# Attention 2 up to unit 93: the value sums of a head pair in one block on TensorE

## Chip, cores and metric

One core of one Trainium2 chip runs the whole program. The metric is device time in microseconds (us) of one execution, the median of several runs.

## What is computed

Two transformer-like layers with adaptive layer norm. Layer 0 is a sliding-window attention and a feed-forward with low-rank updates; layer 1 is a latent attention ("Attention 2" here) and a second feed-forward. The part that matters is the attention of layer 1, with B = 2 batches, S = 512 rows, 128 heads, 4 value columns per head and 64 rope columns:

```
q_c = (c_q @ Wq_up).reshape(b, s, N_HEADS, HEAD_DIM)
q_r = (x @ Wq_rope).reshape(b, s, N_HEADS, ROPE)
scores = (einsum('bqhd,bkhd->bhqk', q_c, k_c) + einsum('bqhd,bkd->bhqk', q_r, k_r)) / scale
attn = softmax(scores, axis=-1)
out = einsum('bhqk,bkhd->bqhd', attn, v_c)
```

## The kernel before

Each engine runs a program of its own, in the order in which it is written, and semaphores tie them together; no scheduler moves anything. Attention 2 works in **units**: unit u is one head pair (two heads) of one batch, pair u // 2, batch u % 2. There are 128 units (UNITS). Up to unit 95 (HALVED = 96) the exponentials of key tiles 0 to 2 are split into two fp16 parts for the value sums; the last key tile stays fp32. From unit 96 on all value sums are fp32.

TensorE's program is a row of **turns**. Turn u holds, in this order (`before_sums`, `behind_sums`):

- the scores of unit u for slots 0 to 3: for each slot a rope matmul (`scores1_rope`, line 2593) and a content matmul (`scores1_content`, line 2600) into bank s % 4. Between them stand `maximum` 0 and 1 (line 2578), which compute approximate scores of unit u + 2, a quarter of a head's queries each, into banks 4 and 5 in turn (their row maxima shift the exponentials later);
- `sum_unit`: the value sums of unit u - 1 into bank 7 (lines 2623 and 2628): 12 matmuls with fp16 data of 512 columns, then 4 with fp32 data of 256 columns. Each matmul writes one of four groups of 32 rows;
- slots 4 to 7 of unit u, `maximum` 2 to 7, and in four pieces the rope queries of unit u + 3 (`queries`, lines 2508 to 2510, 12 matmuls) into bank 6.

In short: 16 score matmuls, 8 of the maxima and 12 of the queries, 36 full ones in each turn, and the block of value sums after the 12th of them. Below r, c, m and q stand for rope, content, maximum and query matmul, so the turn reads r0 c0 r1 c1 r2 c2 r3 m0 c3 m1, the block, r4 c4 m2 q(3) m3 r5 c5 q(3) m4 r6 c6 q(3) m5 r7 c7 m6 q(3) m7.

VectorE (`period`, `maxima`) does in turn u: `q_low` of unit u + 2 (lines 1886 and 1887, the low part of the queries, once ScalarE's `q_high` and so bank 6 are done); then for each of the 8 maxima a reduction over a whole bank (line 1934), after which that bank may be written again; after reductions 4 and 5 `unit_low` (line 1925), the low fp16 part of slots 4 and 5; in even turns after reduction 1 the high part of rope weights (line 1807); at the end a transpose (line 1946). TensorE's side of the two banks is one wait in `max_scores`:

```
wait(pe, max_done, 8 * w + i - 1)
pe.matmul(bank[4 + i % 2][:], q2[:, k % 4, h, i % 4:S:4], km[:, b, h], ...).then_inc(max_mm, 1)
```

So maximum 2 waits until reduction 0 of the same turn is done. `unit_low` waits for the exponential of the slot that follows next:

```
dve.wait_ge(exp1, 8 * u + s + 6)
```

ScalarE does `q_high` (lines 1373, 1374), the 8 exponentials (line 1413), the high fp16 part of slots 4 and 5 (line 1420) and of slots 2 and 3 (line 1424), and in even turns the copy of bank 7 to `ost` (line 1408). GpSimd does both fp16 parts of slots 0 and 1, the low part of slots 2 and 3 (lines 923, 925, 934), three-part bf16 values (`values`, lines 905 to 915) and in even turns the low part of the rope weights (line 850). SyncE issues the DMAs of each turn.

`pv1` counts value sums that are done, `p_split` and `p_low` the fp16 parts, `exp1` the exponentials.

Of the kernel before, what the change touches and what calls it, by code (L numbers as in the profile page):

```python
# [34 lines left out]
UNITS = PAIRS * B  # L35
# [36 lines left out]
def adaln_two_layers(nc, a, out):  # L72
# [8 lines left out]
    with ctx:  # L81
# [638 lines left out]
        def _(pool):  # L720
# [176 lines left out]
            def values(v, k, pair):  # L897
# [5 lines left out]
                wait(pool, pv1, v - 1)  # L903
# [13 lines left out]
            def halve(u, k, pair):  # L917

                par = k % 2
                for i in range(2):  # L920
                    pool.wait_ge(exp1, 8 * u + 5 + i)
# [6 lines left out]
                if k % 2 == 0:  # L928
                    split_rope_weights(pair(4), (k // 2) % 2)
                if not (isinstance(u, int) and u == HALVED - 1):  # L930
                    values(u + 1, k + 1, pair(1))
                pool.wait_ge(exp1, 8 * u + 9)
# [10 lines left out]
            values(0, 0, 0)  # L943
            for u in range(6):
                turn(u, u % 4, lambda n, u=u: (u + n) // 2)
# [145 lines left out]
        def _(act):  # L1091
# [284 lines left out]
            def period(u, k, pair):  # L1376
# [11 lines left out]
                for s in range(8):  # L1388
# [20 lines left out]
                    if exists(u, UNITS):  # L1409
                        in_place = s in IN_PLACE and exists(u, HALVED)  # L1410
                        act.wait_ge(scores1, 8 * u + s + 1)
                        wait(act, pv1, u - 1)
# [8 lines left out]
                    if s == 3 and exists(u, HALVED):  # L1421
                        act.wait_ge(exp1, 8 * u + 8)
                        for i in (2, 3):
# [726 lines left out]
        def _(pe):  # L2150
# [450 lines left out]

            def sum_unit(w, k, pair):

                if exists(w, UNITS):
# [6 lines left out]
                    if isinstance(w, int) and w == 0:  # L2611
                        pe.wait_ge(gate_ready, 6)
                    halved = exists(w, HALVED)
                    apart = isinstance(w, int) and w >= DIRECT
                    opens, closes = apart or k % 2 == 0, apart or k % 2 == 1
                    rows = lambda group: bank[7][32 * group:32 * group + 32, :]
                    if halved:
                        pe.wait_ge(p_split, 4 * w + 4)
                        pe.wait_ge(p_low, 2 * w + 2)
                        for kb in range(HTILES):  # L2620
                            for h in range(2):
                                for half in range(2):
                                    pe.matmul(rows(2 * h + half), vpb[:, k % 2, kb, h], halved_part(k % 2, SLOTS.index((h, kb)), half),  # L2623
                                              start=(kb == 0 and opens), stop=False)
                        for h in range(2):
                            for half in range(2):
                                at = slice(half * S // 2, (half + 1) * S // 2)
                                e = pe.matmul(rows(2 * h + half)[:, at], vp[:, k % 2, HTILES, h], PT[k % 2][:, SLOTS.index((h, HTILES)), at],  # L2628
                                              start=False, stop=closes)
# [296 lines left out]
```

## Time and profile before

| what | us |
|---|---|
| runs, median of 3 | 2178.25 (2177.45 to 2180.17) |
| profiled execution, its own time | 2175.61 |
| span of the profiled execution | 2173.8 |
| TensorE busy | 2122.4 (98%) |
| VectorE, ScalarE, GpSimd busy | 1732.3, 1341.9, 1357.7 |

Turns with fp16 value sums run from about 828 to 1757 us. A matmul's row has the start at which it entered the array and a modelled end; the time that one costs is the distance to the next start. A row "x8" merges instructions that follow each other.

### The profile page before, as it was taken

The page shows a single profiled execution, that of the slowest core. Times are in us where ns is not written, and L with a number is a line of the kernel's source. Part 1 is how long each engine was busy: PE and PEld are TensorE (multiplying, and loading weights), DVE is VectorE, ACT ScalarE, POOL GpSimd, SP SyncE. Part 2 cuts the span into 40 slices and gives each one's busy share as a digit, 9 for nine tenths or more (in the row PEclk, how much of TensorE's full clock was granted, in tenths as well). Part 3 has the DMA queues.
Part 4 walks back from the last instruction along what each step waited for, and adds up shares of the span by engine and source line. Part 5 has one row for each costly group of instructions (what it writes and reads, how often), then busy time and mean ns, then how long its engine had stood idle before and what let it go on. Part 6 is the DMA issues. An engine that isn't in the chain of part 4 may idle for free.

```text
span 2173.8 us, 42824 instructions
## 1 busy us (share of the span) xinstructions
PE 2122.4 (98%) x11276; PEld 1644.1 (76%) x11276; DVE 1732.3 (80%) x3095; ACT 1341.9 (62%) x2709; POOL 1357.7 (62%) x1621
## 2 busy tenths in 40 slices
PE   7999999999999999999999999999999999999978
PEld 4788888888886757777777777777777777777756
DVE  6787788788777758888888888888888877788764
ACT  2443443433433568888888888888888865555532
POOL 4766766766753447777777777777777721365334
PEclk9999999999999999999999999999999999999999
DMA  7010010010004153222222222222222222444441
GB/s 249 26 43 30 20 48 29 19 48 29 19 20 121 37 189 108 71 73 78 74 78 65 77 78 74 76 66 79 75 77 69 75 79 76 138 130 124 114 130 40
DMA packets 138991, 165.82 MB, mean 76 GB/s; under 512 B 30261, under 2 KB 72917, under 8 KB 138916
## 3 DMA queue, kind: packets, MB, share of 16 engines
q1 hardware_dynamic: 135076, 152.31, 24.5%
q0 software_dynamic: 3840, 12.59, 2.0%
q8 instruction: 37, 0.61, 0.1%
q14 instruction: 38, 0.31, 0.0%
HBM read 101.52 MB, written 29.10 MB: 60 GB/s over the span
## 4 chain that ended last, share of the span: by engine, by line
PE 87%; DVE 7%; issue 2%; ACT 1%; POOL 1%; SPq 1%; DMA 1%; DVEq 0%; ACTq 0%; POOLq 0%
PE bank L2593 12%; PE bank L2578 11%; PE bank L2600 11%; PE bank L2155 7%; PE bank L2157 7%; PE bank L2156 7%; PE bank L2510 6%; PE bank L2508 5%; PE bank L2509 5%; PE bank L2623 3%; PE bank L2633 3%; PE bank L2628 2%; DVE rope_b L1631 1%; DVE rope_a L1630 1%; DVE rope_b L1632 1%
## 5 line engine op out<-in xcount | busy, mean ns | idle before, releaser
L1934 DVE TENSOR_REDUCE mcol<-bank 128x1 fp32r<-128x512 f32 x1024 | 684.1, 687 | 186.8 <-PE bank L2578 176.7
L2593 PE MATMUL bank<-q,k 128*128 128x512 f32 x1024 | 417.9, 408 | 0.0
L2578 PE MATMUL bank<-km,q 128*128 128x512 f32 x1024 | 406.0, 397 | 3.5 <-ACT q L1374 2.5
L2600 PE MATMUL bank<-q,k 128*128 128x512 f32 x1024 | 404.0, 395 | 0.0
L2578 PEld LDWEIGHTS bank<-km,q 128*128 128x128 f32 x1024 | 317.6, 310 | 53.0 <-DVE mcol L1934 3.9
L1413 ACT ACTIVATE pT<-bank 128x512 f32<-128x512 f32 x416 | 228.1, 602 | 113.7 <-PE bank L2600 111.9
L1413 ACT ACTIVATE x<-bank 128x512 f32<-128x512 f32 x416 | 227.7, 601 | 88.7 <-PE bank L2600 86.5
L2593 PEld LDWEIGHTS bank<-q,k 128*128 128x128 f32 x1024 | 192.3, 188 | 84.7 <-issue 27.9
L2600 PEld LDWEIGHTS bank<-q,k 128*128 128x128 f32 x1024 | 192.9, 188 | 31.7
L2510 PE MATMUL bank<-hT_hi,wr_lo 128*128 128x512 f32 x512 | 205.5, 401 | 0.0
L2508 PE MATMUL bank<-hT_hi,wr_hi 128*128 128x512 f32 x512 | 202.3, 395 | 0.1
L2509 PE MATMUL bank<-hT_lo,wr_hi 128*128 128x512 f32 x512 | 202.1, 395 | 0.0
L850 POOL TENSOR_TENSOR wr_lo<-wst,wr_hi 128x512 fp32r<-128x512 f32 x64 | 82.5, 1289 | 131.1 <-DVE wr_hi L1807 131.1
L2155 PE MATMUL bank<-hT_hi,w_hi 128*128 128x512 f32 x376 | 150.3, 400 | 0.0
L2157 PE MATMUL bank<-hT_hi,w_lo 128*128 128x512 f32 x376 | 148.5, 395 | 0.0
L2156 PE MATMUL bank<-hT_lo,w_hi 128*128 128x512 f32 x376 | 148.4, 395 | 0.0
L744 POOL TENSOR_TENSOR bq_lo<-rope_a,bq_hi 128x512 fp32r<-128x512 f32 x64 | 83.3, 1302 | 82.0 <-ACT bq_hi L1145 82.0
L923 POOL CAST pH<-x 128x512 f16<-128x512 f32 x96 | 58.8, 612 | 118.6 <-ACT x L1413 118.6
L736 POOL TENSOR_TENSOR rope_a<-rope_a,rope_b 128x512 f32<-128x512 f32 x80 | 105.8, 1323 | 43.2 <-DVE rope_b L1632 43.2
L1925 DVE TENSOR_TENSOR pH_late<-bank,pH_late 128x512 f16<-128x512 f32 x192 | 131.3, 684 | 1.5
L1413 ACT ACTIVATE bank<-bank 128x512 f32<-128x512 f32 x192 | 112.0, 583 | 19.7 <-PE bank L2600 19.7
L925 POOL TENSOR_TENSOR pH<-x,pH 128x512 f16<-128x512 f32 x96 | 117.8, 1227 | 7.7
(372 smaller groups left out, 5061.5 us busy)
## 6 DMA issues: line engine op xcount, KB each, us to landing
q<-q SPq DMA_DIRECT2D x256, 128.0 KB, 2.3
wst<-in_L_attn_Wq_rope SPq DMA_DIRECT2D x64, 256.0 KB, 3.1
o_d<-ost SPq DMA_DIRECT2D x63, 256.0 KB, 3.1
st_q<-in_L_attn_wq SPq DMA_DIRECT2D x8, 1024.0 KB, 7.6
st_wo<-in_L_attn_wo SPq DMA_DIRECT2D x8, 1024.0 KB, 5.4
q<-qc_d SPq DMA_DIRECT2D x256, 32.0 KB
km<-kc_d SPq DMA_DIRECT2D x256, 32.0 KB
k<-kc_d SPq DMA_DIRECT2D x256, 32.0 KB
```

The source lines that it names most:

```text
L1413: act.activation(bank[s % 4][:] if in_place else PT[k % 2][:, s], bank[s % 4][:], ACT.Exp, scale=float((HD1 + ROPE) ** -0.5)).then_inc(exp ...
L1925: dve.tensor_tensor(halved_part(k % 2, s, 1), bank[s % 4][:], halved_part(k % 2, s, 0), ALU.subtract).then_inc(p_low, 1)
L1934: dve.tensor_reduce(mcol[:, k % 2, i % 4, i // 4:i // 4 + 1], bank[4 + i % 2][:], AX.X, ALU.max, negate=True)\
L2155: pe.matmul(ps, lh_, rh, start=(i == 0), stop=False)
L2156: pe.matmul(ps, lh_, rl, start=False, stop=False)
L2157: e = pe.matmul(ps, ll, rh, start=False, stop=(i == n - 1))
L2508: pe.matmul(bank[6][:], wr_hi[:, par, kk], hT_hi[:, kk, at], start=(kk == 0), stop=False)
L2509: pe.matmul(bank[6][:], wr_hi[:, par, kk], hT_lo[:, kk, at], start=False, stop=False)
L2510: e = pe.matmul(bank[6][:], wr_lo[:, par, kk], hT_hi[:, kk, at], start=False, stop=(kk == KT - 1))
L2578: pe.matmul(bank[4 + i % 2][:], q2[:, k % 4, h, i % 4:S:4], km[:, b, h], start=True, stop=True).then_inc(max_mm, 1)
L2593: pe.matmul(bank[s % 4][:], k1[:, k % 2, t], q1[:, k % 4, h], start=True, stop=False)
L2600: pe.matmul(bank[s % 4][:], k2[:, k % 2, h, t], q2[:, k % 4, h], start=False, stop=True).then_inc(scores1, 1)
```

## The change

Up to turn 94 TensorE has no block of value sums in odd turns. In even turns `sum_pair` sums units u - 2 and u - 1 together: both units' fp16 matmuls, then both units' fp32 ones, with one wait on each semaphore in front. From turn 95 on `sum_unit` works as before. The other engines follow: exponentials of slots 0 to 3 wait for GpSimd's splits in place of `pv1`, and what writes into an fp16 part or a value tile waits for the last pair block. In even turns ScalarE does the high part of slots 2 and 3 behind slot 5 in place of behind slot 3. GpSimd does the rope weights first in even turns, then, after the pair block, the splits, then the values of both units. VectorE's and SyncE's code is not touched.

```diff
--- before.py
+++ after.py
@@ -900,7 +900,7 @@
                 full = vc[:, TB * kp:TB * kp + TB, bass.ds(pair * 8, 8)].rearrange("p t (h d) -> p t h d", h=2)
                 src = full[:, 0:HTILES]
                 first, second, third = (vpb[:, kp, 0:HTILES, :, OROWS * kp + i * HD1:OROWS * kp + i * HD1 + HD1] for i in range(3))
-                wait(pool, pv1, v - 1)
+                wait(pool, pv1, v - kp)
                 pool.sem_inc(spare, 1)
                 pool.tensor_copy(first, src).then_inc(vp_ready, 1)
                 pool.tensor_copy(vp[:, kp, HTILES:TB, :, OROWS * kp:OROWS * kp + HD1], full[:, HTILES:TB])
@@ -917,7 +917,10 @@
             def halve(u, k, pair):
 
                 par = k % 2
+                if par == 0:
+                    split_rope_weights(pair(4), (k // 2) % 2)
                 for i in range(2):
+                    wait(pool, pv1, u - par)
                     pool.wait_ge(exp1, 8 * u + 5 + i)
                     pool.sem_inc(spare, 1)
                     pool.tensor_copy(halved_part(par, i, 0), PT[par][:, i]).then_inc(p_split, 1)
@@ -925,11 +928,10 @@
                     e = pool.tensor_tensor(halved_part(par, i, 1), PT[par][:, i], halved_part(par, i, 0), ALU.subtract)
                     if i == 1:
                         e.then_inc(p_split, 1)
-                if k % 2 == 0:
-                    split_rope_weights(pair(4), (k // 2) % 2)
-                if not (isinstance(u, int) and u == HALVED - 1):
+                if par == 0 and not (isinstance(u, int) and u == 0):
+                    values(u, k, pair(0))
                     values(u + 1, k + 1, pair(1))
-                pool.wait_ge(exp1, 8 * u + 9)
+                pool.wait_ge(exp1, 8 * u + (9 if par else 11))
                 for i in range(2, 4):
                     e = pool.tensor_tensor(halved_part(par, i, 1), PT[par][:, i], halved_part(par, i, 0), ALU.subtract)
                 e.then_inc(p_split, 1)
@@ -941,6 +943,7 @@
             pool.wait_ge(vc_ready, NT)
             pool.wait_ge(zeroed, 7)
             values(0, 0, 0)
+            values(1, 1, 0)
             for u in range(6):
                 turn(u, u % 4, lambda n, u=u: (u + n) // 2)
             with pool.Fori(1, LOOP // 4) as g:
@@ -1409,7 +1412,12 @@
                     if exists(u, UNITS):
                         in_place = s in IN_PLACE and exists(u, HALVED)
                         act.wait_ge(scores1, 8 * u + s + 1)
-                        wait(act, pv1, u - 1)
+                        if not exists(u, HALVED):
+                            act.wait_ge(pv1, u - 1)
+                        elif s < 4:
+                            wait(act, p_split, 4 * u - 4)
+                        else:
+                            wait(act, pv1, u - k % 2)
                         act.activation(bank[s % 4][:] if in_place else PT[k % 2][:, s], bank[s % 4][:], ACT.Exp,
                                        scale=float((HD1 + ROPE) ** -0.5)).then_inc(exp1, 1)
                         if in_place:
@@ -1418,8 +1426,9 @@
                                     act.wait_ge(c_stored[i], CONTENT_DMAS[i] * KT)
                             act.wait_ge(exp1, 8 * u + s + 5)
                             act.activation(halved_part(k % 2, s, 0), bank[s % 4][:], ACT.Copy)
-                    if s == 3 and exists(u, HALVED):
+                    if s == (3 if k % 2 else 5) and exists(u, HALVED):
                         act.wait_ge(exp1, 8 * u + 8)
+                        wait(act, pv1, u - k % 2)
                         for i in (2, 3):
                             act.activation(halved_part(k % 2, i, 0), PT[k % 2][:, i], ACT.Copy)
 
@@ -2599,6 +2608,41 @@
                     t = slice(kb * P, (kb + 1) * P)
                     pe.matmul(bank[s % 4][:], k2[:, k % 2, h, t], q2[:, k % 4, h], start=False, stop=True).then_inc(scores1, 1)
 
+            def sum_rows(group):
+                return bank[7][32 * group:32 * group + 32, :]
+
+            def halved_sums(k, opens):
+
+                for kb in range(HTILES):
+                    for h in range(2):
+                        for half in range(2):
+                            pe.matmul(sum_rows(2 * h + half), vpb[:, k % 2, kb, h], halved_part(k % 2, SLOTS.index((h, kb)), half),
+                                      start=(kb == 0 and opens), stop=False)
+
+            def rest_sums(k, closes):
+
+                for h in range(2):
+                    for half in range(2):
+                        at = slice(half * S // 2, (half + 1) * S // 2)
+                        e = pe.matmul(sum_rows(2 * h + half)[:, at], vp[:, k % 2, HTILES, h], PT[k % 2][:, SLOTS.index((h, HTILES)), at],
+                                      start=False, stop=closes)
+                return e
+
+            def sum_pair(u, k, pair):
+
+                if exists(u - 2, UNITS):
+                    pe.wait_ge(exp1, 8 * u + 4)
+                    pe.wait_ge(vp_ready, VP_STEPS * u)
+                    wait(pe, o_copied, pair(-2))
+                    if isinstance(u, int) and u == 2:
+                        pe.wait_ge(gate_ready, 6)
+                    pe.wait_ge(p_split, 4 * u)
+                    pe.wait_ge(p_low, 2 * u)
+                    halved_sums(0, True)
+                    halved_sums(1, False)
+                    rest_sums(0, False)
+                    rest_sums(1, True).then_inc(pv1, 2)
+
             def sum_unit(w, k, pair):
 
                 if exists(w, UNITS):
@@ -2608,29 +2652,17 @@
                         wait(pe, o_copied, pair)
                     elif isinstance(w, int) and w == UNITS - 1:
                         pe.wait_ge(o_copied, PAIRS)
-                    if isinstance(w, int) and w == 0:
-                        pe.wait_ge(gate_ready, 6)
                     apart = isinstance(w, int) and w >= DIRECT
                     opens, closes = apart or k % 2 == 0, apart or k % 2 == 1
...
+                    if exists(w, HALVED):
                         pe.wait_ge(p_split, 4 * w + 4)
                         pe.wait_ge(p_low, 2 * w + 2)
...
+                        halved_sums(k, opens)
+                        e = rest_sums(k, closes)
                     else:
                         for s in range(8):
                             h, kb = SLOTS[s]
...
                     e.then_inc(pv1, 1)
 
             def scores(u, k, pair, slots):
@@ -2654,7 +2686,10 @@
                 maximum(*turn, 0)
                 scores1_content(turn[0], turn[1], 3)
                 maximum(*turn, 1)
-                sum_unit(turn[0] - 1, turn[1] - 1, turn[2](-1))
+                if isinstance(turn[0], int) and turn[0] > HALVED - 2:
+                    sum_unit(turn[0] - 1, turn[1] - 1, turn[2](-1))
+                elif turn[1] % 2 == 0:
+                    sum_pair(*turn)
 
             def behind_sums(*turn):
 
```

**TensorE, the middle of an odd turn in the loop.** Rope and content are rows of q1,k1 and q2,k2, the maxima rows of km,q2 (bank4 is m0 and m2, bank5 m1). Before:

```order
L2578 MATMUL bank4<-km,q2 128x512
L2600 MATMUL bank3<-q2,k2 128x512
L2578 MATMUL bank5<-km,q2 128x512
...
L2623 MATMUL bank7<-pH,vp 32x512 x8
L2623 MATMUL bank7<-pH_late,vp 32x512 x4
L2628 MATMUL bank7<-x,vp 32x256 x4
...
L2593 MATMUL bank0<-q1,k1 128x512
L2600 MATMUL bank0<-q2,k2 128x512
...
L2578 MATMUL bank4<-km,q2 128x512
```

and now, from the same m0 to the same m2:

```order
L2587 MATMUL bank4<-km,q2 128x512
L2609 MATMUL bank3<-q2,k2 128x512
L2587 MATMUL bank5<-km,q2 128x512
...
L2602 MATMUL bank0<-q1,k1 128x512
L2609 MATMUL bank0<-q2,k2 128x512
...
L2587 MATMUL bank4<-km,q2 128x512
```

The second use of bank 4 follows the first after four other matmuls, where the block stood between them before.

**TensorE, the block of an even turn now** (pH and pH_late are the fp16 parts, x and pT the fp32 exponentials of the two units):

```order
L2619 MATMUL bank7<-pH,vp 32x512 x8
L2619 MATMUL bank7<-pH_late,vp 32x512 x4
L2619 MATMUL bank7<-pH,vp 32x512 x8
L2619 MATMUL bank7<-pH_late,vp 32x512 x4
L2627 MATMUL bank7<-x,vp 32x256 x4
L2627 MATMUL bank7<-pT,vp 32x256 x4
```

It holds two blocks' matmuls between one entry and one exit.

**ScalarE, the second half of an even turn.** Before, the copies of slots 2 and 3 (pH<-x x2) stand ahead of slot 4:

```order
L1424 ACTIVATE pH<-x 128x512 x2
...
L1408 ACTIVATE ost<-bank7 128x512
...
L1413 ACTIVATE bank1<-bank1 128x512
...
L1420 ACTIVATE pH_late<-bank1 128x512
...
L1413 ACTIVATE x<-bank2 128x512
```

and now between slot 5 and the exponential of slot 6:

```order
L1411 ACTIVATE ost<-bank7 128x512
...
L1421 ACTIVATE bank1<-bank1 128x512
...
L1428 ACTIVATE pH_late<-bank1 128x512
...
L1433 ACTIVATE pH<-x 128x512 x2
...
L1421 ACTIVATE x<-bank2 128x512
```

The exponential of slot 6 is two instructions later on its engine.

## Rows read from the trace of the kernel before

**Rows 1.** Busy time in the stretch of fp16 turns; columns named in the view.
```profile
core 0: us, PE busy (x) PEld busy (x) DVE busy (x) ACT busy (x) POOL busy (x), PEclk, DMA share, GB/s
828.25:1746.75 918.50, 918.50 (x5265) 717.63 (x5264) 792.33 (x1268) 761.94 (x1362) 693.95 (x1081) 1.00 0.28 75
```

**Rows 2.** Timeline, TensorE, around two blocks: start us, length us, what.
```profile
1199.68 0.61 PE L2623 MATMUL bank<-pH,vp 128*32 128x512 f16 x8
...
1205.17 0.39 PE L2578 MATMUL bank<-km,q 128*128 128x512 f32 x1
...
1209.14 0.40 PE L2578 MATMUL bank<-km,q 128*128 128x512 f32 x1
1209.46 0.62 PE L2623 MATMUL bank<-pH,vp 128*32 128x512 f16 x8
1209.91 0.39 PE L2623 MATMUL bank<-pH_late,vp 128*32 128x512 f16 x4
1210.12 0.60 PE L2628 MATMUL bank<-pT,vp 128*32 128x256 f32 x8
1210.66 0.50 PE L2593 MATMUL bank<-q,k 128*128 128x512 f32 x1
...
1211.24 0.39 PE L2578 MATMUL bank<-km,q 128*128 128x512 f32 x1
```

**Rows 3.** Chain of work that ended last, at a block: start us, us on it.
```profile
1209.54 0.76 PE bank L2623 x12
1210.30 0.43 PE bank L2628 x8
1210.73 0.43 PE bank L2593
```

**Rows 4.** Timeline, VectorE, from reduction 5 of a turn to the next turn's start.
```profile
1205.60 0.69 DVE L1934 TENSOR_REDUCE mcol<-bank 128x1 fp32r<-128x512 f32 x1
1206.21 0.68 DVE L1925 TENSOR_TENSOR pH_late<-bank,pH_late 128x512 f16<-128x512 f32 x1
1206.81 1.28 DVE L1934 TENSOR_REDUCE mcol<-bank 128x1 fp32r<-128x512 f32 x2
1208.12 0.41 DVE L1946 STREAM_TRANSPOSE mrow<-mcol 128x128 f32<-128x128 f32 x1
1208.56 0.68 DVE L1886 TENSOR_TENSOR q<-bank,q 64x512 fp32r<-64x512 f32 x1
1209.26 0.69 DVE L1887 TENSOR_TENSOR q<-bank,q 64x512 fp32r<-64x512 f32 x1
1209.99 1.29 DVE L1934 TENSOR_REDUCE mcol<-bank 128x1 fp32r<-128x512 f32 x2
1211.31 0.43 DVE L1807 CAST wr_hi<-wst 128x512 fp32r<-128x512 f32 x1
```

**Rows 5.** Timeline near the end of Attention 2: a maximum that waits for a reduction.
```profile
2062.10 1.29 DVE L1934 TENSOR_REDUCE mcol<-bank 128x1 fp32r<-128x512 f32 x2 [1.21 <-PE bank L2578]
...
2062.84 0.31 PEld L2578 LDWEIGHTS bank<-km,q 128*128 128x128 f32 x1 [0.52 <-DVE mcol L1934]
2062.84 0.63 PE L2578 MATMUL bank<-km,q 128*128 128x512 f32 x1
...
2063.31 0.39 PE L2593 MATMUL bank<-q,k 128*128 128x512 f32 x1
```

**Rows 6.** Timeline, ScalarE, in an even turn.
```profile
1210.33 1.15 ACT L1424 ACTIVATE pH<-x 128x512 f16<-128x512 f32 x2
...
1213.05 0.58 ACT L1413 ACTIVATE bank<-bank 128x512 f32<-128x512 f32 x1
1213.66 0.60 ACT L1420 ACTIVATE pH_late<-bank 128x512 f16<-128x512 f32 x1
```

**Rows 7.** Timeline, GpSimd, in the same even turn: first, wr_lo and last instruction.
```profile
1209.00 0.61 POOL L923 CAST pH<-x 128x512 f16<-128x512 f32 x1 [2.52 <-ACT x L1413]
...
1212.72 1.29 POOL L850 TENSOR_TENSOR wr_lo<-wst,wr_hi 128x512 fp32r<-128x512 f32 x1
...
1215.33 2.29 POOL L934 TENSOR_TENSOR pH<-x,pH 128x512 f16<-128x512 f32 x2
```

**Rows 8.** Busy time and clock in a stretch of layer 0 with TensorE idle at times.
```profile
666.00:680.00 14.00, 9.91 (x50) 7.89 (x50) 8.66 (x22) 4.26 (x13) 7.44 (x6) 1.00 0.73 275
```

More of the change, by code:

```diff
@@ L2610, in sum_unit @@
                         pe.wait_ge(o_copied, PAIRS)
-                    if isinstance(w, int) and w == 0:
-                        pe.wait_ge(gate_ready, 6)
-                    halved = exists(w, HALVED)
                     apart = isinstance(w, int) and w >= DIRECT
                     opens, closes = apart or k % 2 == 0, apart or k % 2 == 1
-                    rows = lambda group: bank[7][32 * group:32 * group + 32, :]
-                    if halved:
+                    if exists(w, HALVED):
                         pe.wait_ge(p_split, 4 * w + 4)
                         pe.wait_ge(p_low, 2 * w + 2)
[L2620 to L2629, printed above, removed]
+                        halved_sums(k, opens)
+                        e = rest_sums(k, closes)
                     else:
@@ L2632, in sum_unit @@
                             h, kb = SLOTS[s]
-                            e = pe.matmul(rows(2 * h + kb % 2), vp[:, k % 2, kb, h], PT[k % 2][:, s], start=(s < 4 and opens), stop=(s >= 4 and closes))
+                            e = pe.matmul(sum_rows(2 * h + kb % 2), vp[:, k % 2, kb, h], PT[k % 2][:, s], start=(s < 4 and opens), stop=(s >= 4 and closes))
                     e.then_inc(pv1, 1)
```

## The prediction

> **What bounds the kernel now.** I began with the busy table by stretch. In the fp16 turns TensorE is busy for all of 918.50 us, at full granted clock (1.00, the 2.4 GHz level); VectorE has 792.33, or 86% of it, ScalarE 83% and GpSimd 76% [rows 1]. So TensorE sets the pace of this stage, with VectorE close behind, and what the change is worth is read from TensorE's distances between starts.
>
> Next, TensorE's timeline. From one block of value sums to the next it is 1209.46 - 1199.68 = 9.78 us, one turn [rows 2]. From m5 at 1205.17 to m1 at 1209.14 lie 17 full matmuls, 3.97 us, so one costs 0.2335. The 36 of a turn make 8.41, which leaves 1.37 for the block. The chain says the same at the block itself: 0.76 for the fp16 matmuls, 0.43 for the fp32 ones, and 0.43 in place of 0.23 for the r4 behind them, 1.39 in all [rows 3]. Of this the work itself is 1210.12 - 1209.46 = 0.66 and 0.43 [rows 2, 3]. The other 0.28 to 0.30 is a price for entering and leaving the block, paid once per block: a late first load, and a slow restart of the full-width matmuls.
>
> Last, VectorE's timeline over the border of two turns. Reduction 5 starts at 1205.60, 0.43 after its maximum m5 [rows 2, 4]. From there VectorE never waits: unit_low, reductions 6 and 7, the transpose, two halves of q_low, reductions 0 and 1 follow on each other's heels. Reduction 0 starts at 1209.99 and takes 0.69, so it ends at 1210.68, 5.51 us after m5 started. In the same turn m2, which needs that bank, started at 1211.24 [rows 2]. The slack was 0.56 us. It is this slack that the change touches.
>
> **The change, part by part.**
>
> *The pair block.* It holds two blocks' work and one entry and exit: 1.38 + 0.66 + 0.43 = 2.47 us in place of 2 x 1.38 = 2.76. Gain 0.29 per pair. All of it lies on TensorE's path. The bounds: nothing, if the fp16 and fp32 halves of the second unit pay an entry of their own (0.29 again), and 0.30 by the chain's figures. I take 0.29, because inside the old block the fp32 part starts right when the fp16 part is through (0.45 and 0.21 us between the three starts of rows 2, which is 12 matmuls in 0.66 with no gap).
>
> *The odd turn loses its block, and with it 1.38 us between m1 and r4.* VectorE's code is the same, so its chain from m5 of the even turn to the end of reduction 0 of the odd one remains 5.51 us. On TensorE m5 to m2 is now 20 matmuls (r7 c7 m6, three q, m7, r0 to c2, r3 m0 c3 m1, r4 c4) with nothing else between: 20 x 0.2335 = 4.67. So m2 must wait. How long such a wait is, the end of Attention 2 shows: reduction 0 starts at 2062.10, ends 0.69 later at 2062.79, and m2 starts at 2062.84, with VectorE named as its releaser; the next matmul starts 0.47 behind it and not 0.23, because the weights of m2 are only loaded then [rows 5]. So the price is 5.51 + 0.05 - 4.67 = 0.89 of waiting and 0.47 - 0.23 = 0.24 of restart, together **1.13 us per odd turn**. After it TensorE runs free: m3 comes 0.93 + 0.24 behind, reduction 1 ends 0.60 after reduction 0, and m5 and VectorE keep their old distance. In the even turn the block of 2.47 stands between m1 and m2, and m2 has more slack than before.
>
> *Bounds of that price.* From below: the weights could be loaded during the wait, 0.24 less, so 0.89. Less than that, down to nothing, needs a shorter chain on VectorE, whose instructions do not change. From above: the chain starts late. Its second link, unit_low of slot 5, needs the exponential of slot 6, and in even turns ScalarE now has the two copies of slots 2 and 3 ahead of that. From the start of exponential 5: 0.61 to the second fp16 copy, 0.60 for it, 1.15 for the two moved copies, 0.58 for exponential 6, together 2.94 us [rows 6]. VectorE wants it 10 matmuls after (c5 to m5, 2.33) plus 0.61 (reduction 5), also 2.94 us [rows 4]. This falls level. I take zero, and let the bound be 0.3 us.
>
> *GpSimd.* It gets later starts, not more work. One unit is 8.62 us from 1209.00 to 1217.62, with 1.29 for wr_lo [rows 7], so 7.33 without it and 14.7 for two. In an even turn wr_hi is ready at 4.70 us after r0: reduction 0 starts at 2.95 (m5 + 4.82, less the 8 matmuls from m5 to r0, 1.87), reduction 1 ends 1.29 later, the cast takes 0.43 [rows 4]. wr_lo ends at about 6.1, both units are split at 20.8. The next pair block is due one pair of turns (20.4) plus 2.4 later, at 22.8. So 2.0 us of slack: hidden. If that cover were gone, each microsecond over it would be a microsecond per pair.
>
> *ScalarE and SyncE.* ScalarE waits in even turns for the block's end (2.47 + 2.4 = 4.9 us into the turn) and then does `ost` and slot 4, whose scores arrive 0.6 later; its total work is unchanged. The exponentials of slots 0 to 3 are written before the block ends, as they now wait for the splits only. SyncE's queue issues the same transfers in the same order, and by the code each is used about a turn or more after its issue. Zero for both.
>
> *Sum.* Each pair: + 1.13 - 0.29 = + 0.84 us, 19.56 becoming 20.40. There are 47 pair blocks (turns 2 to 94), but turn 0 ahead of the first odd turn holds late gate matmuls as well, which give VectorE time; I let that pair cost nothing (an estimate, worth 0.8 us at most). So 46 x 0.84 = 38.6 us. The profiled execution took 2175.61 (span 2173.8) and becomes 2214.2. The median of the runs, 2178.25, lies 2.6 above it; there I expect **2217 us**, 1.8% slower.
>
> **The rivals.**
>
> *The wait does not bite: faster.* If VectorE's chain from m5 to the end of reduction 0 took 4.6 us or less instead of 5.51, m2 would go straight on and only the 0.29 remained: 47 x 0.29 = 13.6, so 2164.6 us. For it: the slack today is 0.56, and no row of this stage shows such a wait. Against it: the chain has no idle row in it, and 1.38 us are taken out of a path with 0.56 to spare. Chance 7%. That losses and gains meet (a stall of only 0.3 us) has 3%.
>
> *The moved copies make it worse.* If exponential 6 comes 0.3 us late, unit_low and everything behind it shift, and the pair costs 0.84 + 0.30 = 1.14: 46 x 1.14 = 52, so 2231 us. It decides from the first tenth, as the sum above is level. Chance 14%.
>
> *GpSimd becomes the bound.* With 2 us more in its chain than its rows add up to, the pair block waits for `p_split`. A late arrival by 1 us gives 46 x 1.84 = 85, so 2263 us. For it speaks that nothing of its two turns' work but wr_lo can start before the pair block; against it the 2.0 us of slack. Chance 3%.
>
> *The clock drops.* In the stretch around 670 us TensorE was idle for 4.1 of 14 us and the granted clock stayed 1.00 [rows 8]. Were it to fall to the 1.2 GHz level for a whole turn of each pair, 8.41 us would be added 47 times, near 400 us and 2610 in all. The Trainium skill, page "TensorE: Matmul & The Clock Gate", section "A second HAM failure mode: psum-queue depth-cycling", speaks against this change: a matmul stream that cycles through PSUM banks and idles briefly and often can swing between the two clock levels. By that rule the time would be this rival's; the stretch above had such gaps and does not bear it out. Chance 1%.
>
> *That the change doesn't do what it says* has no room: TensorE's order shows the two blocks merged and the odd turn without one.
>
> **How the numbers follow.** The forecast case, a wait of about 0.9 plus the restart in each odd turn, has 72%; the rivals 7, 3, 14, 3 and 1. The likeliest case gives 2217. Its own bounds are 0.60 to 1.0 per pair: 28 to 46 us, 2206 to 2224. To leave out no more than 2 in 10 the range takes in the moved copies above (2231) and, below, 0.07 us less per pair than the lower bound (3 us): **2203 to 2231**. A measurement of this kernel tells 0.2% (4.4 us) from no change. Faster by more than that: 7%. Within it: 2% (a stall that just eats the gain). Slower: 91%.
>
> **What the profile after should show.** TensorE's fp16 rows in groups of 24 every 20.4 us; from the first fp16 matmul of a block to r4 2.3 us. In odd turns a wait at m2 for VectorE's line 1934, about 46 times and 0.5 to 0.9 us each, with a 0.47 step behind it. VectorE's idle before reduction 2 stays, that before reductions 3 and 4 as well. TensorE's share of busy time falls below 98%, the clock stays 1.00. The forecast is wrong if m2 in odd turns follows c4 by 0.23, or if the waits are at the block (GpSimd) or at r1 (`p_low`).

## The result and the profile after

The changed kernel ("after") takes **2214.81 us** (median; 2213.9 to 2215.68) against 2177.45 for the kernel before in the same session (2174.46 to 2180.17). The ratio is 1.0177, 95% interval 1.0163 to 1.0191: slower by 1.8%, far outside the 0.2% that can be told from no change. The forecast was 2217, with 2203 to 2231 around it. The profiled execution of after took 2214.41 (span 2212.6), 38.8 us more in the span than before's 2173.8. One run of one version below (experiment 3) took 5962.57 us, was slow, and is left out of the comparison.

First the busy table of the stretch of fp16 turns of after; columns as in [rows 1].

```profile
828.00:1785.00 957.00, 923.06 (x5268) 722.24 (x5267) 797.13 (x1269) 760.42 (x1366) 684.57 (x1080) 1.00 0.27 72
```

In [rows 1] TensorE had no idle microsecond in 918.50. Now it is idle for 957.00 - 923.06 = 34 us, at an unchanged granted clock of 1.00 (2.4 GHz). What it waits for, the view of TensorE's waits says (us in total, times, longest), here for 828 to 1757 us:

```profile
PE bank L2587 <- DVE mcol L1943: 32.9, 45, 0.7
```

The same view of before has no row in that stretch. L2587 is `maximum` and L1943 is the reduction (L2578 and L1934 before). In the shares of the chain that ended last, TensorE went from 87% to 71% and VectorE from 7% to 14%:

```profile
PE 71%; DVE 14%; issue 6%; ACT 5%; DMA 1%; POOL 1%; SPq 1%; DVEq 0%; ACTq 0%; POOLq 0%
```

Where it happens is in TensorE's timeline of after over one pair of turns (start, length, what). These rows answer to [rows 2].

```profile
1203.48 0.40 PE L2587 MATMUL bank<-km,q 128*128 128x512 f32 x1
1203.81 0.62 PE L2619 MATMUL bank<-pH,vp 128*32 128x512 f16 x8
...
1205.55 0.60 PE L2627 MATMUL bank<-pT,vp 128*32 128x256 f32 x8
1206.08 0.50 PE L2602 MATMUL bank<-q,k 128*128 128x512 f32 x1
1206.41 0.40 PE L2609 MATMUL bank<-q,k 128*128 128x512 f32 x1
...
1210.36 0.39 PE L2587 MATMUL bank<-km,q 128*128 128x512 f32 x1
...
1214.34 0.39 PE L2587 MATMUL bank<-km,q 128*128 128x512 f32 x1
1214.57 0.40 PE L2602 MATMUL bank<-q,k 128*128 128x512 f32 x1
1214.80 0.39 PE L2609 MATMUL bank<-q,k 128*128 128x512 f32 x1
1215.92 0.62 PE L2587 MATMUL bank<-km,q 128*128 128x512 f32 x1 [0.73 <-DVE mcol L1943]
1216.38 0.39 PE L2517 MATMUL bank<-hT_hi,wr_hi 128*128 128x512 f32 x1
...
1224.17 0.62 PE L2619 MATMUL bank<-pH,vp 128*32 128x512 f16 x8
```

Block to block is 1224.17 - 1203.81 = 20.36 us, where two turns of before took 2 x 9.78 = 19.56 (medians of all pairs: 20.35 and 19.55). A block stands after m1, the tenth full matmul of its turn; the description of the kernel before says the 12th, but its own list r0 to m1 has ten. The first matmul of the pair block to r4 is 2.27. In the odd turn m1, r4 and c4 follow at matmul distance, and then m2 starts 1.12 us behind c4 and the next matmul 0.46 behind m2, in place of 0.23 and 0.23. That is 0.89 and 0.23, or 1.12 us too much per odd turn. (The weights of m2 are loaded from 1215.92 on, at its own start, and those of the matmul behind it from 1216.13 on.) The bracket names 0.73 us of idle time only: c4's modelled end takes up part of the distance, so the distance between starts is the number to sum, not the idle column.

VectorE's timeline of the same turns answers to [rows 4]:

```profile
1210.79 0.69 DVE L1943 TENSOR_REDUCE mcol<-bank 128x1 fp32r<-128x512 f32 x1
1211.40 0.68 DVE L1934 TENSOR_TENSOR pH_late<-bank,pH_late 128x512 f16<-128x512 f32 x1
1212.00 1.28 DVE L1943 TENSOR_REDUCE mcol<-bank 128x1 fp32r<-128x512 f32 x2
1213.31 0.41 DVE L1955 STREAM_TRANSPOSE mrow<-mcol 128x128 f32<-128x128 f32 x1
1213.75 0.69 DVE L1895 TENSOR_TENSOR q<-bank,q 64x512 fp32r<-64x512 f32 x1
1214.45 0.69 DVE L1896 TENSOR_TENSOR q<-bank,q 64x512 fp32r<-64x512 f32 x1
1215.17 2.10 DVE L1943 TENSOR_REDUCE mcol<-bank 128x1 fp32r<-128x512 f32 x3
```

It is the chain of before, link by link, with no idle time in it: m5 at 1210.36 to reduction 0 at 1215.17 is 4.81 us (4.82 before), and with the reduction's 0.69 it ends at 1215.86. m2 starts 0.06 behind that.

The two engines whose work was moved kept up. ScalarE does the two moved copies (L1433) ahead of exponential 6:

```profile
1209.57 1.14 ACT L1433 ACTIVATE pH<-x 128x512 f16<-128x512 f32 x2
1210.62 1.25 ACT L1421 ACTIVATE x<-bank 128x512 f32<-128x512 f32 x2
```

and `unit_low`, which wants that exponential, still starts 0.61 behind its reduction (1210.79 and 1211.40). The row x2 of 1210.62 is exponentials 6 and 7; the first of them ends at 1211.20, 0.20 ahead of `unit_low`. GpSimd in the same pair, its first and last row:

```profile
1206.21 1.30 POOL L850 TENSOR_TENSOR wr_lo<-wst,wr_hi 128x512 fp32r<-128x512 f32 x1 [4.69 <-DVE wr_hi L1816]
...
1219.66 2.30 POOL L936 TENSOR_TENSOR pH<-pT,pH 128x512 f16<-128x512 f32 x2
```

It is through at 1221.96, and the next pair block starts at 1224.17: 2.2 us of slack.

One wait of after was in no step of the prediction. TensorE's timeline behind the last pair block:

```profile
1784.26 0.40 PE L2587 MATMUL bank<-km,q 128*128 128x512 f32 x1
1786.47 0.61 PE L2619 MATMUL bank<-pH,vp 128*32 128x512 f16 x8 [1.81 <-POOL pH L936]
```

and GpSimd's in the same place:

```profile
1783.95 2.27 POOL L936 TENSOR_TENSOR pH<-x,pH 128x512 f16<-128x512 f32 x2
```

Unit 94 has a block of its own in turn 95, one turn behind the pair block and not two. GpSimd did rope weights, both parts of slots 0 and 1 of unit 94 and both units' values ahead of unit 94's low parts of slots 2 and 3, and ends those at 1786.22, 0.25 before the block starts. The block starts 2.21 behind m1 and not 0.33, once. The bill closes: 46 x (20.36 - 19.56) + 1.9 = 38.7 us, of 38.8. (Two small items are left out of it and cancel: the first odd turn's 0.3, and one more block's gain of 0.3, as 47 blocks are merged.)

### The profile page after: what moved, and what is told of

It is laid out like the page before. It is cut to its first block, busy times and chain, and to the rows that moved or that the text cites. A ratio compares the mean times of both kernels' runs of the same rounds, so it can differ in the third digit from the quotient of the medians.

```text
span 2212.6 us, 42692 instructions
## 1 busy us (share of the span) xinstructions
PE 2125.5 (96%) x11276; PEld 1648.4 (74%) x11276; DVE 1736.7 (78%) x3095; ACT 1338.9 (61%) x2709; POOL 1348.4 (61%) x1621
## 4 chain that ended last, share of the span: by engine, by line
PE 71%; DVE 14%; issue 6%; ACT 5%; DMA 1%; POOL 1%; SPq 1%; DVEq 0%; ACTq 0%; POOLq 0%
PE bank L2587 9%; PE bank L2602 8%; PE bank L2609 7%; PE bank L2164 7%; PE bank L2166 7%; PE bank L2165 7%; DVE mcol L1943 4%; PE bank L2519 4%; PE bank L2518 4%; PE bank L2517 4%; PE bank L2619 3%; PE bank L2665 3%; ACT pH L1433 2%; PE bank L2627 2%; DVE q L1895 1%
## 5 line engine op out<-in xcount | busy, mean ns | idle before, releaser
L1943 DVE TENSOR_REDUCE mcol<-bank 128x1 fp32r<-128x512 f32 x1024 | 684.0, 687 | 223.8 <-PE bank L2587 208.3
L2587 PE MATMUL bank<-km,q 128*128 128x512 f32 x1024 | 417.3, 408 | 37.8 <-DVE mcol L1943 34.5
L2587 PEld LDWEIGHTS bank<-km,q 128*128 128x128 f32 x1024 | 317.8, 311 | 106.4 <-DVE mcol L1943 57.8
L1934 DVE TENSOR_TENSOR pH_late<-bank,pH_late 128x512 f16<-128x512 f32 x192 | 131.2, 683 | 1.5
L1428 ACT ACTIVATE pH_late<-bank 128x512 f16<-128x512 f32 x192 | 114.6, 597 | 6.1
L928 POOL TENSOR_TENSOR pH<-x,pH 128x512 f16<-128x512 f32 x96 | 112.2, 1169 | 7.7
```

Of the source, the lines that this page charges most:

```text
L1934: dve.tensor_tensor(halved_part(k % 2, s, 1), bank[s % 4][:], halved_part(k % 2, s, 0), ALU.subtract).then_inc(p_low, 1)
L1943: dve.tensor_reduce(mcol[:, k % 2, i % 4, i // 4:i // 4 + 1], bank[4 + i % 2][:], AX.X, ALU.max, negate=True)\
```

## The experiments

**1. The wait for reduction 0 taken away by order.** Odd turns 1 to 93 issue m2 and m3 five matmuls later and m4 one later, among the same matmuls; m5 to m7 keep their places, and nothing is added or left out. (`turn[1] % 2` is the parity of the turn.)

```diff
+                if turn[1] % 2 == 1 and (not isinstance(turn[0], int) or 0 < turn[0] < HALVED - 2):
+                    scores(*turn, (4, 5))
+                    queries(*turn, 0)
+                    maximum(*turn, 2)
+                    queries(*turn, 1)
+                    maximum(*turn, 3)
+                    scores1_rope(turn[0], turn[1], 6, turn[2](0))
+                    maximum(*turn, 4)
+                    scores1_content(turn[0], turn[1], 6)
+                    queries(*turn, 2)
+                    maximum(*turn, 5)
+                    scores(*turn, (7,))
+                    maximum(*turn, 6)
+                    queries(*turn, 3)
+                    maximum(*turn, 7)
+                    return
```

> The changed kernel, with TensorE's order in the second half of the odd turns 1 to 93 rearranged: r4 c4 r5 c5 q(3) m2 q(3) m3 r6 m4 c6 q(3) m5 and then as before, so that m2 and m3 come 1.17 us later and m4 0.23 us later; the same instructions and the same waits. Theory (VectorE's chain from m5 to the end of reduction 0 stalls m2): the chain of 5.56 us is met by 25 matmuls, 5.84 us, the wait and its restart are gone, a pair takes 20.36 - 1.13 = about 19.25 us and the whole 2214.8 - 46 x 1.1 = 2164 us, under the kernel before. Rival 1 (the loss lies in the pair block or in what ScalarE and GpSimd do around it): the odd turns' order is of no account, 2215 us. Rival 2 (VectorE is simply full in an odd turn of 8.4 us, so it stalls wherever the maxima stand): the wait moves to m4 or m5 and half or more of the loss stays, 2190 us or more.

Measured: **2168.9 us** (2167.03 to 2171.38), ratio to the kernel before 0.9967 (0.9956 to 0.9978). TensorE's waits from 828 to 1787 us hold one row, the one of unit 94:

```profile
PE bank L2619 <- POOL pH L936: 2.1, 1, 2.1
```

and its timeline goes from block to block in 1222.63 - 1203.33 = 19.30 us:

```profile
1203.33 0.61 PE L2619 MATMUL bank<-pH,vp 128*32 128x512 f16 x8
...
1222.63 0.61 PE L2619 MATMUL bank<-pH,vp 128*32 128x512 f16 x8
```

All 46 waits at m2 are gone, and the time is 46 us shorter. So the loss was the wait at m2, and the block's gain is real: 19.30 (19.32 in the median of all pairs) is 0.26 below the pair of before.

The expectation was 2164, with 19.25 us for a pair. Most of the 5 us between is a small wait that the new order brings with it. VectorE's timeline and TensorE's at the end of a rearranged turn:

```profile
1219.01 0.68 DVE L1943 TENSOR_REDUCE mcol<-bank 128x1 fp32r<-128x512 f32 x1
...
1219.91 0.46 PE L2587 MATMUL bank<-km,q 128*128 128x512 f32 x1
1220.21 0.43 PE L2602 MATMUL bank<-q,k 128*128 128x512 f32 x1
1220.47 0.39 PE L2609 MATMUL bank<-q,k 128*128 128x512 f32 x1
```

This is reduction 5, which m7 waits for, and it ends at 1219.69; m7 (1219.91) has its weights loaded from 1219.75 on. m7 to r0 is 0.30 and r0 to c0 0.26, in place of 0.23 each. Over all rearranged turns that is 0.09 us in the median, 0.10 in the mean, and nothing in the other turns. In the kernel before the load of m7 starts 0.28 behind the end of that reduction, here 0.05 (medians). The wait is too short for the view of waits. 19.55 - 0.33 (the merged block, see below) + 0.10 = 19.32.

**2. VectorE's chain made longer.** If m2 waits for the end of that chain, whatever is added to it must reach the time in the changed kernel, and none of it in the kernel before as long as it stays under the 0.56 of slack. Two kernels add a reduction over 256 columns, whose result nobody reads, ahead of `q_low` in odd turns; one adds two over 512 columns (`(512, 512)` in the loop) to the kernel before.

```diff
+                if k % 2 == 1 and (not isinstance(u, int) or 0 < u < HALVED - 2):
+                    for i, cols in enumerate((256,)):
+                        dve.tensor_reduce(l_pad[:, 40 + i:41 + i], hT_hi[:, 0, 0:cols].bitcast(F32), AX.X, ALU.max)
                 q_low(u + 2, k + 2)
```

In the changed kernel:

> The changed kernel with one more VectorE instruction in front of q_low in the odd turns 1 to 93, a reduction over 256 columns, whose result nobody uses. By the reduction over 512 columns (0.69 us) and half of its streaming it takes an estimated 0.35 to 0.45 us. Theory: it lengthens the chain that m2 waits for, and every bit of it is paid: 47 x 0.4 = 19 us more, 2230 to 2237. Rival (TensorE waits for something else there, and VectorE is only the last that the profile names): under 4 us more.

In the kernel before:

> The kernel before with the same added reduction in the same odd turns. Theory: the slack at m2 is 0.56 us there, the instruction of about 0.4 us fits in it, no change (2177, within 3 us). Rival (VectorE's work costs time wherever it is added, since it is busy 86%): 19 us more.

> The kernel before with two added reductions over 512 columns in the odd turns 1 to 93, about 1.3 us in all. Theory: 0.56 us of it is slack, the rest is waited for at m2, with 0.24 us of restart: 1.3 - 0.56 + 0.24 = 0.98 us in each of 47 turns, 46 us more, about 2223, with waits at m2 as in the changed kernel although the blocks of value sums are those of before. Rival (only the missing block in the odd turn makes the loss): under 10 us more.

Measured: 2222.17 us (2221.57 to 2224.4) in the changed kernel, ratio 1.0214 (1.0197 to 1.0232); 2176.55 (2172.54 to 2179.63) in the kernel before, ratio 1.0001 (0.9991 to 1.001); with the long addition 2214.72 (2211.54 to 2217.07), ratio 1.0175 (1.0158 to 1.0191).

The first missed its number (2230 to 2237 expected), as the instruction was mis-sized. VectorE's timeline in e2:

```profile
1215.20 0.41 DVE L1955 STREAM_TRANSPOSE mrow<-mcol 128x128 f32<-128x128 f32 x1
1215.45 0.36 DVE L1961 TENSOR_REDUCE l_pad<-hT_hi 128x1 f32<-128x256 f32 x1
1215.83 0.68 DVE L1895 TENSOR_TENSOR q<-bank,q 64x512 fp32r<-64x512 f32 x1
```

It takes 0.36, but it starts before the transpose's row ends, so transpose to `q_low` grows from 0.44 to 0.63 only: 0.19 us. The wait grows by just that (0.9 at most in e2, 0.7 in after; waits of 41.6 us in 45 against 32.9), and 46 x 0.19 = 8.7 us is what the time shows within its spread (+ 7.4). In the kernel before the same 0.19 costs nothing. With the long addition the kernel before gets the changed kernel's wait, without any merged block:

```profile
PE bank L2581 <- DVE mcol L1934: 17.4, 45, 0.4
```

Its distance from transpose to `q_low` is 1.49 in place of 0.44, + 1.05. (The expectation of 2223 had 1.3 there and is missed by 8 us for that reason.) The slack of 0.56 eats its part, 0.24 for the restart comes on top: 1.05 - 0.56 + 0.24 = 0.73 per odd turn by the sum. Measured are 10.55 from block to block in the turns with the wait, against 9.78, so 0.77, and 46 x 0.77 = 35 us of the 38 in the time. This is the closest test of the two numbers on which the prediction rests: the slack and the restart.

**3. What in the block is saved.** Two readings of the 0.28 to 0.30 us per block were open: a price for leaving the full-width matmuls and coming back, or one for the change from fp16 to fp32 matmuls. From experiment 1, the parts of the two units alternate (fp16, fp32, fp16, fp32):

```diff
                     halved_sums(0, True)
-                    halved_sums(1, False)
                     rest_sums(0, False)
+                    halved_sums(1, False)
                     rest_sums(1, True).then_inc(pv1, 2)
```

> e1_max_later with the pair block in another order: fp16 and fp32 matmuls of the first unit, then fp16 and fp32 ones of the second. Theory A (the price of a block is paid for entering it from and leaving it to full-width matmuls): the same time, 2169, and the block of 2.27 us from first matmul to r4. Theory B (it is paid for each return from fp32 to fp16 data): 0.1 to 0.3 us more a pair, 2174 to 2183.

Measured: 2169.92 us (2165.65 to 2177.32), ratio 0.9969 (0.9957 to 0.9981), experiment 1's time. The profiled execution is one of its longer ones (2175.42), but in it too a pair takes 19.32 us (median). TensorE's timeline in the block:

```profile
1207.38 0.61 PE L2619 MATMUL bank<-pH,vp 128*32 128x512 f16 x8
...
1208.03 0.61 PE L2627 MATMUL bank<-x,vp 128*32 128x256 f32 x8
1208.47 0.60 PE L2619 MATMUL bank<-pH,vp 128*32 128x512 f16 x8
...
1209.11 0.60 PE L2627 MATMUL bank<-pT,vp 128*32 128x256 f32 x8
1209.65 0.50 PE L2602 MATMUL bank<-q,k 128*128 128x512 f32 x1
```

First matmul to r4 is 2.27, the same as with one change of type. So the type costs nothing; entering and leaving does. The Trainium skill, page "TensorEngine Tiling (Array Packing)", section "Key Properties", says that a change of tiling mode drains TensorE; the rows agree in that the price, 0.3 us, is at the two borders alone: 0.10 more than a full matmul from m1 to the block, 0.10 at the block's end (0.54 from the start of the last fp32 row to r4, and 0.44 from the other one to the next part) and 0.10 from r4 to c4. No run here shows what TensorE does in that time.

Then the second unit's sums were put two matmuls behind the first's, behind r4 and c4:

```diff
                     halved_sums(0, True)
-                    halved_sums(1, False)
                     rest_sums(0, False)
+
+            def sum_second(u):
+
+                if exists(u - 2, UNITS):
+                    halved_sums(1, False)
                     rest_sums(1, True).then_inc(pv1, 2)
...
+                if turn[1] % 2 == 0 and (not isinstance(turn[0], int) or turn[0] < HALVED - 1):
+                    sum_second(turn[0])
```

> e1_max_later with the pair block cut in two: the first unit's sums in their place, the second unit's behind r4 and c4 of the same even turn, so that two entries and exits are paid again while VectorE, ScalarE and GpSimd do what they do in e1_max_later. Theory (0.29 us per entry and exit): 47 x 0.29 = 13.6 us more, 2182 to 2183. Rival (the merged block saves nothing; e1_max_later is faster for another reason): 2169.

Measured: 2191.17 us (2188.67 to 2194.77), ratio 1.0069 (1.0052 to 1.0085): 22.3 us over experiment 1, 0.47 per pair, where some 0.29 was expected. TensorE's timeline:

```profile
1215.56 0.61 PE L2619 MATMUL bank<-pH,vp 128*32 128x512 f16 x8
...
1216.76 0.50 PE L2602 MATMUL bank<-q,k 128*128 128x512 f32 x1
1217.09 0.40 PE L2609 MATMUL bank<-q,k 128*128 128x512 f32 x1
1217.42 0.62 PE L2619 MATMUL bank<-pH,vp 128*32 128x512 f16 x8
...
1218.61 0.62 PE L2587 MATMUL bank<-km,q 128*128 128x512 f32 x1
1219.07 0.39 PE L2517 MATMUL bank<-hT_hi,wr_hi 128*128 128x512 f32 x1
```

The first unit's part takes 1.20 to r4 in place of 1.09 to the second part (experiment 3's rows), c4 to the block is 0.33, and m2 to the next is 0.46: 0.11, 0.10 and 0.23 more. (r4 to c4 has its 0.10 in experiment 1 too.) In sum 0.44, and from pair to pair the medians give the same, 19.76 against 19.32. What is left of the 0.47 lies outside the pairs. The direction of the expectation held, its size was taken for an exit into r4. Here the exit is into a maximum, m2, and the weight load of a maximum is the longest of any full matmul of a turn: in the costliest groups of after's page

```profile
L2587 PEld LDWEIGHTS bank<-km,q 128*128 128x128 f32 x1024 | 317.8, 311 | 106.4 <-DVE mcol L1943 57.8
L2602 PEld LDWEIGHTS bank<-q,k 128*128 128x128 f32 x1024 | 192.4, 188 | 65.1 <-issue 47.3
```

it takes 311 ns against 188 ns, 0.12 us more, and the exit into m2 costs 0.13 more than the one into r4. (A maximum's weights are every fourth query, `i % 4:S:4`. That this stride makes its load longer was not tested.)

**4. Is the new order itself worth something?** The rearranged odd turns in the kernel before, blocks as they were:

> The kernel before (one block per unit) with the rearranged second half of the odd turns of e1_max_later. Theory: m2 has 0.56 us to spare there and waits for nothing, so a later place buys nothing: 2176, no change within 0.2%; what e1_max_later has under the kernel before is then the merged block's 0.29 us a pair and not the new order. Rival (the new order is good by itself): 2169 as e1_max_later.

Measured: **2189.34 us** (2187.07 to 2191.7), ratio 1.0064 (1.0047 to 1.0081). A miss: I had expected no change. VectorE's timeline in an even turn:

```profile
1216.24 1.29 DVE L1934 TENSOR_REDUCE mcol<-bank 128x1 fp32r<-128x512 f32 x2
1217.56 1.35 DVE L1807 CAST wr_hi<-wst 128x512 fp32r<-128x512 f32 x1
1218.83 2.08 DVE L1934 TENSOR_REDUCE mcol<-bank 128x1 fp32r<-128x512 f32 x3
```

The cast of `wr_hi` takes 1.35 us, and 0.43 in [rows 4]; the three reductions behind it are late, and m4 waits (0.43 to the next matmul and not 0.23, in each even turn). With m7's 0.09 in the odd turns that is 0.29 per pair, and the pair measures 19.83 against 19.55 (medians). GpSimd at that time:

```profile
1217.46 1.17 POOL L925 TENSOR_TENSOR pH<-x,pH 128x512 f16<-128x512 f32 x1
```

GpSimd's subtraction starts 0.10 ahead of the cast and lasts until 1218.63; the cast ends 0.28 behind that. So it is in all 47 casts of the stretch: they start 0.10 to 0.20 behind a subtraction's start and end 0.28 to 0.29 behind its end. In the kernel before the order is the other way round: the cast starts at 1211.31 and the subtraction at 1211.49, the cast takes 0.43, and the subtraction 1.26:

```profile
1211.49 1.26 POOL L925 TENSOR_TENSOR pH<-x,pH 128x512 f16<-128x512 f32 x1
```

By these rows the cast waits for the subtraction's end, while a subtraction behind a cast is 0.09 longer. This was tested by moving the cast to where GpSimd has nothing else to do:

```diff
-                        if i == 1 and k % 2 == 0:
+                        if i == 3 and k % 2 == 0:
                             split_rope_weights(p, (k // 2 - 1) % 2, quad)
```

> The kernel before with the odd turns rearranged (as in e5_max_later_before), and in even turns VectorE's cast of wr_hi behind reduction 3 in place of reduction 1. There the cast took 1.35 us and started 0.10 us behind GpSimd's subtraction of 1217.46 (1.17 us); 0.43 us where it starts ahead of one. Theory A, the two cannot run at once and the cast waits for the end of the subtraction: behind reduction 3, at about 1218.9, GpSimd has nothing to do but wait for this cast, so it takes 0.43 us, nothing is late behind it, the waits of m4 go, and the run takes 2176 to 2180 us. Theory B, the order of the odd turns itself costs the 13 us (the later queries and maxima hand VectorE a late start in even turns): the cast may be short, but the run stays near 2189.

The cast, as expected, is short again:

```profile
1218.44 0.43 DVE L1807 CAST wr_hi<-wst 128x512 fp32r<-128x512 f32 x1
```

and from 828 to 1757 us the waits of weight loads for VectorE, of which e5 (the run without the later cast) has

```profile
PEld bank L2578 <- DVE mcol L1934: 11.4, 47, 0.3
```

have no row in e10 (the run with it). The Trainium skill, page "SBUF — State Buffer", section "Who interferes with whom", gives the rule: VectorE's copies and casts within SBUF can take a second port that GpSimd uses too, and whichever starts first blocks the other for its whole instruction. The rows agree for the cast: 1.35 when it starts second, 0.43 when it starts first or alone. For the subtraction they bear it out less: it starts with 0.25 us of the cast still to run and is 0.09 longer.

The time, though, was 2187.85 us (2185.36 to 2190.35), ratio 1.0051 (1.0031 to 1.007), and not 2176 to 2180. Over the stretch of fp16 turns 95 turns took 941.8 us in e5 and 934.7 in e10 (928.6 in the kernel before), so there the cast gave back 7 of 13 us. Six are left, and they are m7's wait for reduction 5, as in experiment 1: 0.12 in the median of the rearranged turns. Behind the stretch the late cast costs 4 of the 7 us again, as the edit moved it in every even turn. From the last fp16 matmul to the last maximum e10 takes 311.8 us, and every other version 307.5 to 308.0; weight loads of maxima wait there for VectorE's reductions 12 times, 5.8 us in all, and 4 times, 1.4 us, in e5. Up to the first fp16 block e10 took 1.9 us more than e5; versions with the same code there differ by up to 4 us, so this shows nothing. What experiment 4 does say: the rearrangement is no gain of its own. Experiment 1 is faster than the kernel before because of the merged block.

**5. The last wait.** On top of experiment 1, GpSimd does in turn 94 unit 94's values and low parts first, and rope weights and unit 95's values behind them:

```diff
+                last = isinstance(u, int) and u == HALVED - 2
-                if par == 0:
+                if par == 0 and not last:
...
-                    values(u + 1, k + 1, pair(1))
+                    if not last:
+                        values(u + 1, k + 1, pair(1))
...
+                if last:
+                    split_rope_weights(pair(4), (k // 2) % 2)
+                    values(u + 1, k + 1, pair(1))
```

> e1_max_later, and GpSimd in turn 94 alone does the splits of unit 94 and its values first, then the rope weights and the values of unit 95. Theory: in turn 95 the block of the single unit 94 comes one turn and not two after its splits could begin, and TensorE waits once for GpSimd, 1.8 us in the changed kernel, 2.1 us in e1_max_later; this wait goes: about 2167, which is within the measurement's spread, but the trace shows no wait of a value sum for GpSimd. Rival: the wait moves to the rope queries of turn 95, which need the weights' low part.

Measured: **2165.58 us** (2164.53 to 2168.58), ratio 0.9959 (0.9945 to 0.9973), the lowest median of the study. The times alone do not tell it from experiment 1 (0.9956 to 0.9978); the trace does: the view of waits has no row for TensorE from 828 to 1800 us, so the wait is gone and has not moved to the rope queries. Against experiment 1 the span is 2.5 us shorter (2162.7 and 2165.2), of which the wait was 2.1.

## Why the prediction was right

By its own steps:

- **The pair block, 2.47 and a gain of 0.29.** Right, slightly low. From m1 to c4 the kernel before takes 1.86 us per turn (1209.14 in [rows 2] to c4 at 1211.00), 3.72 per pair. After, it is 1206.41 - 1203.48 = 2.93 in the even turn, m1 at 1203.48 being the matmul ahead of the block, and 0.46 in the odd one, 3.39. The gain is 0.33. Less the 0.46 of two full matmuls, the pair block is 2.47, as forecast, and the single block 1.40 and not 1.38. Experiment 3 showed why: one entry and exit less, whatever the types.
- **The wait of m2, 1.13 per odd turn.** Measured 1.12. The prediction read the chain at the border from an odd to an even turn, and the one that stalls is from even to odd; it is the same there (before: reduction 5 at 1215.38, reduction 0 at 1219.76, 4.38 us, and 4.39 in [rows 4]). Its parts were the chain of VectorE (5.51 to the reduction's end; 1215.86 - 1210.36 = 5.50), 20 matmuls, and the restart (0.46 - 0.23). Experiment 1 removed it, experiment 2 lengthened it by 0.19 with 0.19 us of work (e2), and made it in the old kernel (e4).
- **Net 0.84 per pair.** Measured 0.80, the difference being the block's gain. 46 pairs make 36.8 us where 38.6 stood.
- **The first pair at nothing.** Nearly: in turn 1 the next matmul comes 0.46 behind m2 and m2 0.32 behind c4, 0.3 us.
- **ScalarE's copies level, GpSimd 2.0 us of slack.** `unit_low` kept its 0.61, and the slack is 2.2. The rival of the moved copies (14%) fell with the first, that of GpSimd (3%) with the second. ScalarE's sum was not quite level: it added the lengths of rows, 2.94 from the start of exponential 5 to the end of exponential 6, and the rows overlap at their ends, so it took 2.73 (1208.47 to 1211.20) with 0.2 us to spare. That is still a narrow answer and not a safe one.
- **The clock.** 1.00 over the stretch, with a wait of 0.7 us in each odd turn. That rival falls, and with it the rule of the Trainium skill's page "TensorE: Matmul & The Clock Gate" that was set against the trace: in this kernel such gaps did not move the clock.
- **One sign did not come true.** VectorE's idle before reduction 2 was to stay. In odd turns it is gone (0.40 in before, while after has reductions 0 to 2 in one row of 2.10), as m2 itself now waits. It costs nothing.
- **Not in the prediction:** the wait of unit 94's block, 1.9 us. The reckoning of GpSimd's due time was made for a pair block two turns away and not for the one place where the pattern ends. It is what lies between the 36.8 of the pairs and the 38.8 of the span.

The total is nearer than the terms deserve. The sum for the profiled execution was + 38.6 and came out at + 38.8 by two errors that cancel, which is luck: 1.8 too much in 46 pairs, and 1.9 left out for unit 94. The 2.2 us between 2217 and 2214.81 are almost all in the last step: 2.6 us were added for the distance of the profiled execution to the median, and in after that distance is 0.4 (2214.41 and 2214.81).

## What to carry to other kernels

When a block of work is moved from one place to another on the engine that sets the pace, look for the engine that used the time it took. Here a block of 1.38 us was the cover for a VectorE chain with 0.56 us to spare, and the 0.3 us saved per pair brought a wait of 1.1. The remedy was not to undo the merge but to issue the matmul that waits a few places later, with the last unit's wait taken away too: 2165.58 us in place of 2214.81, below the 2176 of the kernel before. Look at the new order in the same way: it left a wait of 0.1 us a few matmuls on, which no view of waits names. And where a repeated pattern is re-timed, cost its first and last instance apart.

## What the runs showed of the hardware

- **A restart at a maximum costs 0.23 us more than the wait**: m2's weights are loaded only when its semaphore comes, so the next matmul is 0.46 behind it (after, 46 times). [rows 5] had one such place.
- **Going from full-width matmuls to 32-column ones and back costs 0.3 us, and 0.43 where the way back is into a maximum**, whose weight load takes 311 ns and not 188 (e7, e8). The data type within the block costs nothing (2.27 us in both orders).
- **VectorE's cast waits for a GpSimd subtraction that started first**: 0.43 us alone or first (before, e10), 1.26 to 1.36 where it starts 0.10 to 0.20 behind (e5, 47 times). A shift of one engine by less than a microsecond can flip that, on another engine, and did so in experiment 4.
- **An instruction can cost half of its row**: the reduction of 0.36 us lengthened VectorE's chain by 0.19 (e2), as it starts ahead of the end of the row before it. Two rows of 1.22 together cost 1.05 (e4).
- **Waits of 0.7 us, one every 20.4 us, left the granted clock at 1.00** (after, 828 to 1785 us, TensorE busy 96%).
